# Two transformer layers on one core: the first chunk's q placed on chip, and written step orders for all engines

## What is computed

```python
xn = layernorm(x)
qkv = xn @ Wqkv                       # 32 heads of 16 for q, one head for k and v
scores = einsum('bqhd,bkd->bhqk', q, k) / 4 + alibi, causal
attn = softmax(scores) @ v            # then @ Wo
delta = top-2-of-4 gated LoRA of xn   # router Wr, A, B
x = x + attn @ Wo + delta
xn = layernorm(x)
x = x + attention1(xn)                # 16x16 scores inside each token
      + ffn(xn)                       # silu(gate) * up, down; int weights with scales, 1792 wide
```

## Time and profile before

| what | value |
| --- | --- |
| runs (three), median and ends | 624.21 us, 623.84 to 625.64 |
| the profiled execution, span | 623.2 us |
| PE busy in it | 570.7 us (92%) |
| DVE busy | 461.3 us (74%) |
| ACT busy | 377.0 us (61%) |
| POOL busy | 351.7 us (56%) |
| granted TensorE clock, mean | 0.959 |

### The profile page before, as it was taken

The page is one execution under the profiler, slowest core; times in us unless marked ns, Lnnn a source line. Parts: engine busy times, 40 slices in busy tenths (PEclk is TensorE's granted clock), DMA queues, the critical chain, the costliest instruction groups (busy, mean ns, idle before and its releaser), DMA issues.

```text
span 623.2 us, 14286 instructions
## 1 busy us (share of the span) xinstructions
PE 570.7 (92%) x5590; PEld 421.3 (68%) x5590; DVE 461.3 (74%) x1034; ACT 377.0 (61%) x703; POOL 351.7 (56%) x364
## 2 busy tenths in 40 slices
PE   4579583699999999999999999999999999999997
PEld 4466451467885668776968587858685876785783
DVE  4769874899999874899697748996986569354642
ACT  3287095847875478675757485858684776651240
POOL 6231595724655667674837574848576677542140
PEclk9987895599999999999999999999999999999999
DMA  8767799905054146001610160016001000000000
GB/s 207 152 95 78 123 237 217 170 2 54 2 54 87 37 68 70 3 4 35 88 17 5 35 86 4 4 35 88 1 5 52 18 1 9 28 2 2 35 1 34
DMA packets 98942, 34.97 MB, mean 56 GB/s; under 512 B 75548, under 2 KB 90044, under 8 KB 98876
## 3 DMA queue, kind: packets, MB, share of 16 engines
q1 hardware_dynamic: 76044, 24.58, 22.7%
q0 software_dynamic: 2352, 7.18, 5.7%
q10 hardware_dynamic: 20480, 2.31, 2.6%
HBM read 30.19 MB, written 8.39 MB: 62 GB/s over the span
## 4 chain that ended last, share of the span: by engine, by line
PE 68%; DVE 13%; SPq 8%; ACT 4%; issue 3%; DMA 2%; POOL 2%; ACTq 1%; DVEq 0%
PE B_bank L1266 27%; PE B_bank L1287 14%; PE A_bank L1218 7%; SPq L693 5%; PE A_bank L1191 4%; DVE mx L1537 4%; PE A_bank L1120 3%; PE E_bank L1176 3%; PE B_bank L1154 3%; PE E_bank L1171 2%; PE B_bank L1254 1%; DMA qq<-nmp 1%; ACTq L693 1%; SPq L731 1%; SPq L717 1%
## 5 line engine op out<-in xcount | busy, mean ns | idle before, releaser
L883 POOL TENSOR_TENSOR probs<-e,probs 128x512 f16<-128x512 f32 x176 | 208.3, 1188 | 127.2 <-ACT probs L999 126.8
L1266 PE MATMUL B_bank<-xs,wgu 128*128 128x256 f16 x1792 | 204.3, 273 | 0.3 <-DVE hf L1649 0.3
L998 ACT ACTIVATE e<-E_bank,wn 128x512 f32<-128x512 f32 x192 | 133.7, 696 | 103.4 <-PE E_bank L1176 53.9
L1266 PEld LDWEIGHTS B_bank<-xs,wgu 128*128 128x128 f16 x1792 | 172.7, 98 | 21.6 <-DVE hf L1649 0.6
L999 ACT ACTIVATE probs<-E_bank,wn 128x512 f16<-128x512 f32 x192 | 134.0, 698 | 0.0
L1287 PE MATMUL B_bank<-wd,hbuf 128*128 128x512 f16 x448 | 99.9, 379 | 0.1
L897 POOL TENSOR_TENSOR hbuf<-hf,hbuf 128x512 f16<-128x512 f32 x56 | 65.8, 1176 | 56.2 <-ACT hbuf L1033 55.8
L1537 DVE TENSOR_REDUCE mx<-B_bank 128x2 f32<-128x384 f32 (+5 forms) x168 | 92.1, 603 | 4.5 <-PE B_bank L1154 4.4
L1639 DVE SCALAR_TENSOR_TENSOR hf<-ebuf,B_bank 128x512 f32<-128x512 f32 x56 | 38.3, 684 | 62.2 <-ACT ebuf L1043 61.9
L1287 PEld LDWEIGHTS B_bank<-wd,hbuf 128*128 128x128 f16 x448 | 43.2, 98 | 49.3 <-POOL hbuf L897 0.6
L1043 ACT ACTIVATE ebuf<-B_bank,sgx 128x256 f32<-128x256 f32 x112 | 47.5, 485 | 22.1 <-PE B_bank L1266 20.8
(11 more groups left out here) (199 smaller groups left out, 696.3 us busy)
## 6 DMA issues: line engine op xcount, KB each, us to landing
qq<-q_parts SPq DMA_DIRECT2D x21, 256.0 KB
x<-in_x SPq DMA_DIRECT2D x20, 256.0 KB, 3.1
out_y<-x SPq DMA_DIRECT2D x16, 256.0 KB, 2.0
xa<-in_x SPq DMA_DIRECT2D x12, 256.0 KB, 5.1
q_parts<-qs SPq DMA_DIRECT2D x48, 64.0 KB, 2.9
wgu<-in_gate_w POOLq DMA_DIRECT2D x4, 448.0 KB, 9.1
wgu<-in_up_w POOLq DMA_DIRECT2D x4, 448.0 KB, 8.7
wd<-in_down_w POOLq DMA_DIRECT2D x4, 448.0 KB, 7.1
```

The costliest lines, as they stand in the source:

```text
L883: pool.tensor_tensor(probs[:, u % PSLOTS, 1, :], e32[:, w, :], probs[:, u % PSLOTS, 0, :], ALU.subtract).then_inc(s_lop, 1)
L998: act.activation(e32[:, w, :], psum("exp", i, g, w)[:, :], ACT.Exp, scale=wn[:, 7:8])
L1266: mm = pe.matmul(psum(name, u, i)[:, a * SEQ:(a + 1) * SEQ].rearrange("p (t n) -> p t n", t=NU), wgu[:, m, k, (2 * i + a) * P:(2 * i + a + ...
```

## The change

Chunk 0's q no longer passes DRAM. SP copies each tile (b, m) from q_first to a staging tile `natural[m]` in three DMAs (step place on SP), and DVE copies 64 rows of it into qq (step place on DVE). The staging tile's other rows are filled once: zeros by DVE (zero), slopes and positions by eight small DMAs (tables on SP), after ACT has scaled them (tables on ACT, before on DVE). Steps store, gather_first, gather(1) and clear are gone. For batch 0 the maxima are reduced tile by tile, 32 reductions of two groups (FIRST_MAXG); they are transposed in two halves (nm0), and added to the scores by extra matmuls with one-hot rows (pick) instead of rows in qq. nmT(0) and nm(0) are gone.

The constants are loaded between the x tiles 1 and 2, the slope and position rows in two DMAs instead of six; a dummy Exp comes first on ACT; the mask writing (masks) is a step apart, behind the identity's copies (tables). wq_turned moves from wgu to xs. The gate and up loads wait for the last place's staging copies, the late loads follow them, Wo's load (wo) follows the last place, and the down loads wait for gather(3). hi and lo take the router's weights first (HI_ORDER). Last, `RANK` is replaced by `QUEUES`: for each engine the names of its steps in their order, written out; `US` has new numbers.

```diff
+FIRST_MAXG = [(tb, 2 * n, 2) for n in range(NK) for tb in range(NTB)]
+HI_ORDER = [NK, 0, 1, 2, 3] + list(range(NK + 1, 2 * NK + 2))
...
+QUEUES = {
+    "PE": """
+        xT0*2 tok norm q0 xT0 norm2 xT0 q0 tok q0 kT*2 max*16 q0 max*2 nm0 q0 max*3 exp max exp max*2 q0 exp*2 q0 exp*2
+        pv exp*2 max*2 exp q0 max*2 pv exp*3 pv midT xT0*2 max*4 tok pv xT0*2 max*2 norm2 max*2 nm0 tok max*2 exp max
+        exp qa exp q max*3 qa max*2 exp*2 max*4 q max*4 exp pv max qa q exp*2 qa q exp pv nmT exp*3 kT pv*2 exp*2 attT*2
...
+    "ACT": """
+        start squares xT0*2 squares*3 tables squares2 xT0*2 q0*3 kT hi*3 kT q0 nm0 q0 hi exp*2 q0 exp*2 mix q0 exp*5 q0
+        hi exp*3 midT xT0*2 squares2*2 xT0*2 nm0 exp*3 hi*3 exp q*2 hi exp*2 hi q exp*2 q exp nmT exp*3 kT exp*2 attT*2
...
+    "DVE": """
+        zero*2 ln0*2 xn0 tables xn0 pick zero*2 ln0*2 xn0 masks norm hot*2 xn0 hot scale hot scaled q0*2 norm2 tok
+        scale2 tok place q0 place max*13 place max*3 hot*2 q0 nm0 max*2 hot*2 max*6 q0 place mix q0 exp mixb q0 exp pv
+        ln0*2 exp q0 ln0*2 place max xn0*2 pv*2 max*2 place*2 xn0 xT0*2 place max exp xn0 max*2 tok pv max*2 xT0*2 max*3
+        nm0 norm2 tok scale2 max*4 exp max*9 q max q setup0 max*4 pv exp q setup1 q pv exp nmT setup3 ln0 exp pv ln0 pv
+        ln0*2 xn0 attT*2 xn0*2 xT0 exp xT0*2 max*5 exp out max pv*2 xn0 max*5 exp max out xT0 ln1 pv exp max ln1 max
...
+    "POOL": """
+        start ln0*2 turn*2 ln0*2 norm turn*2 norm2 lo*4 exp*4 late exp late exp ln0*4 exp*2 ffn_load*8 late*7 lo norm2
+        exp*3 lo setup1 lo*2 exp*3 setup2 exp*2 ln0 lo*2 ln0 exp ln0 exp*2 ln0 exp*5 ln1*2 exp*7 up*2 exp*5 up*2 exp*2
+        ffn_load*4 exp up exp*3 up exp*2 ln0 ln1 ln0 exp*3 up att4 ln1 ln0*2 exp*9 up exp*3 up att4 up exp*7 ln1 up exp
...
+    "SP": """
+        x_load tables place*5 x_load place*3 wo q x1_load*3 q x1_load q x_load q nm gather q*2 nm gather x_load q nm q
...
+            def tables():
+                act.wait_ge(s_rows, 32)
+                act.activation(pos_half, pos_nat, ACT.Copy)
+                act.activation(slope_up, slope_nat, ACT.Copy, scale=POS).then_inc(s_pos, 1)
...
+                for m in range(NK):
+                    for r0, rows in ((R_ALIBI, slope_up), (R_ALIBI + 3, pos_half)):
+                        sp.dma_start(natural[m][r0:r0 + 3, :], rows[m:3 * NK:NK, :]).then_inc(s_natural[m], 16)
...
+            def place(b, m):
+                if b:
+                    sp.wait_ge(s_placed, m + 1)
+                for g, part in enumerate(PART_Q):
+                    if part == 0:
+                        sp.wait_ge(s_q0h, b * NK + m + 1)
+                    else:
+                        wait_used(sp, "q0", b, m)
+                    sp.dma_start(natural[m][g * HD:(g + 1) * HD, :].rearrange("d (h t) -> d h t", t=SEQ),
+                                 q_first[:, b, m, part, :]).then_inc(s_natural[m], 16)
...
                 if n == 2:
-                    pool.wait_ge(s_nmrow[0], 32)
-                    pool.wait_ge(s_wlo, NK + 1)
+                    pool.wait_ge(s_placed, 2 * NK)
+                    pool.wait_ge(s_wlo, 1)
...
                 if n == 0:
-                    pool.wait_ge(s_gather[1], 16 * 3)
+                    pool.wait_ge(s_natural[NK - 1], 32 + 48 * NB)
+                if n == 2 * NK:
+                    pool.wait_ge(s_gather[1], 16 * 4)
...
+                    for c1 in range(0 if i else blocks):
+                        row = g // 2 % 2 * 2 * NTB + 2 * (t0 + c1) + g % 2
+                        mm = pe.matmul(acc[:, c0 + c1, :, :], pick[:, row:row + 1].broadcast_to([NG, P]),
+                                       nm_first[:, g // (NHG // 2), :].rearrange("r (h t) -> r h t", t=GT), start=False, stop=True,
+                                       skip_group_check=True)
...
+            def zero(m):
+                dve.memset(natural[m][R_ZERO:R_HOT, :].bitcast(F32), 0.0).then_inc(s_zero, 1)
...
+            def place(b, m):
+                dve.wait_ge(s_natural[m], 32 + 48 * (b + 1))
+                dve.tensor_copy(qq[0:R_HOT, b, :, 8 * m:8 * m + 8, :],
+                                natural[m][0:R_HOT, :].rearrange("d (h c t) -> d c h t", c=NTB, t=GT)).then_inc(s_placed, 1)
```

More of the change, by code:

```diff
@@ L110 @@
[L110 to L114, removed]
[3 rows of a table removed]
-        "store": (-219, -1, 0, -59), "mix": (-312, -1, 0, 86), "squares": (31.5, -1, 39, 54), "squares2": (-178.5, 4, 40),
[4 rows of a table removed]
[L123 to L130, removed]
-    "POOL": {"start": (338, 0.5, 34, 23), "ffn_load": (-280, 1, 13, 3), "ln0": (468.5, 1, -41, 144), "clear": (-81.5, 2, -1, -103),
-        "turn": (176, 4, -29, 20), "norm": (-170, 1, -10, 39), "late": (244.5, 4, 0, 29), "norm2": (-191, 3, -46, 131),
-        "lo": (520, -2, -13, -11), "setup1": (-258.5, 1, -53), "setup2": (491.5, 3, -40, 154), "exp": (-533, 4),
-        "ln1": (-398, -2, -24, -97), "att4": (416, -2, -81, 153), "up": (-667.5, 0.5, -49, -52)},
-    "SP": {"x_load": (361, 4, 3, 2), "consts": (395, -2, -26, 1), "wo": (438, 2, 247, -23), "gather_first": (-18, 3, -6, -235),
-        "gather": (68, 2, -86, -160), "tables": (142, 1, -7, 41), "q": (952.5, 4, -60, 97), "nm": (211, 1, 0, 264),
-        "x1_load": (-206.5, 2, -14), "down": (215.5, 2, 0, 129)},
@@ new lines, in groups_of @@
+def groups_of(i):
+    return MAXG if i else FIRST_MAXG
+US = {"PE": {"norm": 2.1, "norm2": 0.2, "nmT": 0.15, "nm0": 0.25, "q0": 2.0, "xT0": 0.5, "tok": 2.0, "kT": 0.24, "qa": 1.3,
+             "q": 1.3, "pv": 0.62, "attT": 0.46, "midT": 0.13, "outa": 1.3, "out": 1.74, "xT1": 0.46, "tok1": 1.0,
+             "gate": 1.76, "up": 1.76, "half": 1.74, "half2": 1.74, "half3": 1.74, "down": 0.87},
+      "ACT": {"squares": 0.7, "squares2": 1.2, "hi": 1.36, "nmT": 0.3, "nm0": 0.27, "midT": 0.28, "start": 7.4,
+             "tables": 3.8, "q0": 0.48, "xT0": 0.5, "q": 0.5, "kT": 0.75, "mix": 0.12, "exp": 1.16, "attT": 0.5,
+             "xT1": 0.5, "att2": 0.54, "gate": 0.74, "up": 0.54},
+      "DVE": {"zero": 1.07, "pick": 0.9, "masks": 2.2, "norm": 0.2, "scale": 1.3, "tables": 0.6, "place": 0.7, "nm0": 0.3, "scaled": 0.4, "hot": 0.64,
[4 rows of a table added]
+      "POOL": {"norm": 1.0, "norm2": 0.6, "lo": 1.2, "setup2": 2.2, "start": 2.2, "turn": 1.1, "ffn_load": 0.62,
+             "ln0": 0.9, "ln1": 0.9, "late": 0.68, "setup1": 0.5, "exp": 1.16, "att4": 2.1, "up": 1.18},
+      "SP": {"wo": 1.4, "x_load": 2.4, "tables": 5.0, "q": 0.5, "gather": 2.1, "place": 1.85, "nm": 1.2,
+             "x1_load": 0.5, "down": 0.5}}
@@ L165, in cost, with sequence @@
     return US[engine][step[0]]
-def rank(engine, step):
-    base, by_chunk, first, own = (RANK[engine][step[0]] + (0, 0))[0:4]
-    if step[0] not in BY_BATCH and step[0] not in BY_CHUNK:
-        return base
-    c = step[1] // 2 if step[0] in BY_BATCH else step[1]
-    return base + by_chunk * c + (0 if c else first) + (own if step[1] == (0 if step[0] in BY_BATCH else 1) else 0)
+def sequence(engine, queues):
+    left = {name: list(steps) for name, steps in queues.items()}
+    out = []
+    for word in QUEUES[engine].split():
+        name, _, count = word.partition("*")
+        out += [left[name].pop(0) for _ in range(int(count or 1))]
+    assert not any(left.values()), left
+    return out
 class Plan:
@@ L283, in attention @@
             u = 3 * (i * NHG + g) + w
[L284 removed]
+            p.add("PE", ("exp", i, g, w), *([] if w else [dve("nm0", 0, g // 4)] if i == 0 and g % 4 == 0 else [sp("nm", i, gap=2.8)] if i and g == 0 else []))
             after = [pe("exp", i, g, w)]
@@ L408, in plan @@
     p.add("POOL", ("start",))
+    for m in range(NK):
+        p.add("DVE", ("zero", m))
     for n in range(N_FFN):
-        p.add("POOL", ("ffn_load", n), sp("gather", 1, gap=8.0), at=34.0 + 5.0 * n)
+        p.add("POOL", ("ffn_load", n), *([sp("place", 1, NK - 1, gap=2.5)] if n == 0 else [pool("late", 8), sp("gather", 3, gap=5.0)] if n >= 2 * NK else []))
     for c in range(NCH):
@@ L1045, in gate_ @@
                 sig.then_inc(s_sig, 1)
-            run("ACT", {"start": start, "squares": squares, "squares2": squares2, "hi": hi, "nmT": nmT, "midT": turn_mid, "store": store, "xT0": xT0, "q0": q0, "q": q, "kT": kT, "mix": mix, "exp": exp, "attT": attT,
+            run("ACT", {"start": start, "squares": squares, "squares2": squares2, "hi": hi, "tables": tables, "nm0": nm0, "nmT": nmT, "midT": turn_mid, "xT0": xT0, "q0": q0, "q": q, "kT": kT, "mix": mix, "exp": exp, "attT": attT,
                         "xT1": xT1, "att2": att2, "gate": gate_, "up": up})
```

402 lines of the change are left out of this document (227 added, 175 removed), and 14 rows, old and new, of tables (RANK, US).

## The result

The changed kernel takes 620.73 us (median of 20 runs, 618.86 to 624.68) against 625.25 us of the kernel before (20 runs, 623.5 to 626.8): ratio 0.9935, 95% interval 0.992 to 0.9951. It is faster, by some 4 us and not by the forecast 12. The profiled execution took 619.77 us, its span 617.9 against 623.2.

A forecast was written before the change was run, and what follows sets the result against it. VectorE was taken as the new bound of the start, up to attT(0,0): 623.2 - (123.6 - 107) + 2.5 + 2 = 611.1 us, and with 1.0 for the median 612. The range was 600 to 622.

The forecast's parts named there:

- The start up to the exps: Start of the kernel, batch 0: first nm0 ends at 40 us, first exp on TensorE at 43 instead of 77.78.
- The sum of VectorE's work up to attT: VectorE's work until TensorE turns batch 0's attention output (attT(0,0)): 93.0 us after the change, 88.7 before.
- over 85% busy from 30 to 105: Sign that the forecast is right: VectorE over 85% busy between 30 and 105 us.
- Idle time of VectorE, 14 (7 to 21): Start, up to batch 0's last pv: 14 us idle (5 before x tiles, 3 scale chain, 6 exps), 34.9 before.
- 0 to 3 us for nm(1) and the loads: Start: late x tiles for VectorE and nm(1)'s rows for TensorE cost 0 to 3 us, inside the idle 14.
- Behind attT: After attT(0,0): 2.5 us of TensorE work moved there, and about 2 us more of TensorE waiting for VectorE.
- the collision: First rival: POOL's weight loads collide with chunk 1's q stores in the start; 619 us, chance 0.17.
- 7.6 MB at 181 GB/s: Loads behind the q pieces, from about 61 us: they need 42 us, till about 101, meeting chunk 1's stores.
- Better covered: Rival: VectorE idles only 7 us in the start, with no lag after attT(0,0); 603 us, chance 0.13.
- No effect: Rival: batch 1's exps still wait for nm(1)'s rows behind SP's queue, attT(0,0) stays; 623 to 625 us, chance 0.05.
- slower: Rival: written order stalls TensorE in the body, 3 us per batch gives 636 us; 626 to 640, chance 0.10.
- The matmuls by one-hot rows: Batch 0's 24 exp steps: four more matmuls each, upper bound 9.4 us of TensorE, costed at nothing as covered.

The follow-up runs named there:

- after_copy: Changed kernel with GpSimd's maximum across partitions (setup1) replaced by a plain copy, that maximum left out: 617.0 us, ratio 0.9875 to the kernel before.
- copy_sp: after_copy with the four loads of layer 1's x tiles moved ahead of chunk 1's q stores on SP: 616.0 us, ratio 0.9833 to the kernel before.
- diag_late: Changed kernel, maximum across partitions by TensorE and VectorE instead of GpSimd, gate and up loads behind batch 0's last low half: 634.0 us, 1.0130 of the kernel before.
- diag_behind: Changed kernel, maximum across partitions by TensorE and VectorE, gate and up loads in pairs behind four low halves of batch 1: 622.0 us, 0.9943 of the kernel before.
- diag_nopick: Changed kernel, maximum across partitions by TensorE and VectorE, batch 0's matmuls by one-hot rows left out: 618.8 us, against 619.1 with them.

## Why the prediction was right and wrong

**The start up to the exps: right.** nm0 at 38.06 for 40 (VectorE's work 31.5 for 30.5, its idle time 6.6 for some 10), first exp at 38.84 for 43. The sum of VectorE's work up to attT, 93.0, was 93.8 in the kernel after and 93.7 in after_copy. The sign "over 85% busy from 30 to 105" failed in the kernel after (82%) and holds in after_copy (90%).

**Idle time of VectorE, 14 (7 to 21): the step that failed.** It was 21.1, at the upper bound. The forecast put "6 at ACT and PE in the exps"; the stop at 104.99 alone is 8.37, and 1.58 without the all-reduce. Its cause was not among the steps that the prediction went through. It followed what the change moves on VectorE, ScalarE, TensorE and SP, and of GpSimd only the loads and the low halves of the weights. But moving the exps 39 us forward also moves them past whatever GpSimd did between 39 and 78 us, and there stood setup1; the new list for GpSimd ("exp*3 lo setup1 lo*2 exp*3") shows it between the low halves. In the trace of before its row of 0.38 us with 5.92 and 7.00 us of "issue" on both sides was to be read. With the step in the exps the last pv of batch 0 was ready at 114.70, without it at 107.28: 7.4 of the 7.8 us between the forecast's 107 and attT at 114.84.

**Where it goes on from there.** Without the step VectorE is where the forecast had it, but TensorE then waits for nm(1)'s rows: attT is at 109.0 (after_copy) and, with SP's queue relieved, at 107.9 (copy_sp), near the forecast's 107 once both are gone. The prediction had allowed 0 to 3 us for nm(1) and the loads inside VectorE's idle time; the wait is TensorE's, behind VectorE's last pv, and comes on top.

**Behind attT: +4.5 forecast.** It is +3.5 in the kernel after (503.1 against 499.6; TensorE's work 2.5 more, as forecast, its idle time 0.9 more for 2), +5.9 in after_copy and +7.4 in copy_sp. The earlier attT comes, the more is given back. That is idle time: behind attT TensorE's work is 494.6, 494.9 and 495.0 us in these three, its idle time 8.4, 10.6 and 12.0. Part of it lies before batch 2's first maxima (1.60 and 2.62 us, none in the kernel after), where the kernel waits for gather(2), the end of SP's chain; that the gather is what ends this stop is argued, since the profile shows no releaser there. So 5.8 us at attT were 3.4 in the span and 3.7 in the time. Of the 8.7 us between 612 and 620.7, another part is the base: the sum started from a median of 624.21 in three runs, and twenty gave 625.25.

**The rivals.** The first one, the collision, gave 619, close to the 620.7; its mechanism was wrong. Loads and stores do meet, as the Trainium skill (DMA: Bandwidth & Descriptors, "Issuing engines are not separate DMA queues") says of transfers started by different engines, and the 17.1 us of diag_late agree with it; only not at the place of this change, as diag_behind shows. Its term was mis-sized: 7.6 MB at 181 GB/s were to take till about 101 (61 + 42 would be 103), and they had landed by some 88. That 619 was so near is luck. "Better covered", an idle time of 7, went the other way. "No effect" and "slower" didn't happen: the time moved, and the body's idle TensorE time is 7.2 us for 6.7. The matmuls by one-hot rows were rightly costed at nothing (diag_nopick), and holding the loads behind the pieces, for which no price was given, is worth 14 us.

## What to carry to other kernels

When a change moves a chain of work earlier, list for each engine the steps that the chain now passes in that engine's order, those that the change doesn't touch too, and price each by the time until the engine's next instruction, not by its own length. Idle time marked "issue" on both sides of a short instruction can be time in which the engine is occupied, as here; it costs nothing only as long as nobody queues behind it. Once such a stop is gone, look at the queue that comes next: of 5.8 us won at the end of batch 0 (after_copy), 3.7 were left in the time.
